# Output halves, queries and the turn of the next batch's x change their slots in a hand-written matmul schedule (gated cross-attention with a mixture feed-forward)

## What is computed

```python
q = (_layernorm(x) @ Wq + bq).reshape(B, L, NKV, G, HDIM)        # B=4, L=256, NKV=8, G=4, HDIM=128
k_, v_ = jnp.split(ctx @ Wkv + bkv, 2, axis=-1)                  # Lk=1601
scores = jnp.einsum('blkgd,bmkd->bkglm', q, k) * scale
attn = jax.nn.softmax(scores, axis=-1)
o = jnp.einsum('bkglm,bmkd->blkgd', attn, v).reshape(B, L, NHEAD * HDIM)
x = x + jnp.tanh(g_xattn[0]) * (o @ Wo + bo)
x = x + jnp.tanh(g_ffn[0]) * ffn(_layernorm(x))                  # base + top-2 of 8 LoRA adapters
```

## Time and profile before

| | |
|---|---|
| median of three runs | 2308.6 us |
| the profiled execution, its own time | 2309.07 us |
| its span | 2307.1 us |
| TensorE matmul busy | 2257.9 us, 98% |
| VectorE / ScalarE / GpSimd busy | 1812.2 / 1667.0 / 1631.9 us (79 / 72 / 71%) |
| mean granted TensorE clock | 0.999 |

### The profile page before, as it was taken

The page is one execution under the profiler, slowest core; times in us unless marked ns, Lnnn a source line. Parts: engine busy times, 40 slices in busy tenths (PEclk is TensorE's granted clock), DMA queues, the critical chain, the costliest instruction groups (busy, mean ns, idle before and its releaser), DMA issues.

```text
span 2307.1 us, 37400 instructions
## 1 busy us (share of the span) xinstructions
PE 2257.9 (98%) x12361; PEld 1940.2 (84%) x12361; DVE 1812.2 (79%) x3162; ACT 1667.0 (72%) x3156; POOL 1631.9 (71%) x1372
## 2 busy tenths in 40 slices
PE   7999999999999999999999999999999999999988
PEld 6888888887888888888888888888888888888865
DVE  5888888888787787787778787787788778787785
ACT  4777777776777777777777777777777777777763
POOL 5887886976668678757657778776756756766762
PEclk9999999999999999999999999999999999999999
DMA  7344353564233342325214333333422213222211
GB/s 259 129 158 137 118 162 110 173 202 150 88 113 110 100 159 95 128 87 202 92 49 137 111 128 120 111 130 112 160 83 96 92 60 111 67 98 88 68 66 55
DMA packets 137567, 271.85 MB, mean 118 GB/s; under 512 B 21664, under 2 KB 54944, under 8 KB 137120
## 3 DMA queue, kind: packets, MB, share of 16 engines
q1 hardware_dynamic: 122400, 255.71, 32.7%
q10 hardware_dynamic: 14976, 13.74, 2.6%
HBM read 202.44 MB, written 66.97 MB: 117 GB/s over the span
## 4 chain that ended last, share of the span: by engine, by line
PE 80%; DVE 9%; POOL 4%; issue 3%; ACT 3%; DMA 0%; ACTq 0%; SPq 0%; POOLq 0%; DVEq 0%
PE psW L419 12%; PE psW L420 12%; PE psW L421 12%; PE psS L419 7%; PE psS L421 7%; PE psS L420 7%; PE psW L616 7%; PE psW L617 6%; PE psW L618 6%; PE psW L475 3%; DVE psum_ L1309 3%; DVE mrun L1274 2%; POOL xs L805 2%; PE psW L483 1%; DVE pl L1053 1%
## 5 line engine op out<-in xcount | busy, mean ns | idle before, releaser
L805 POOL TENSOR_TENSOR xs<-xs,mb 128x512 f32<-128x512 f32 (+1 forms) x832 | 1067.8, 1309 | 475.6 <-ACT mb L876 475.6
L1274 DVE TENSOR_TENSOR mrun<-psS,mrun 128x512 f32<-128x512 f32 (+1 forms) x704 | 482.4, 685 | 339.5 <-ACT xs L876 338.3
L876 ACT ACTIVATE xs<-psS 128x512 f32<-128x512 f32 (+1 forms) x832 | 496.2, 597 | 242.6 <-PE psS L421 230.9
L1053 DVE TENSOR_TENSOR pl<-psP,ph 128x512 fp32r<-128x512 f32 (+1 forms) x672 | 459.2, 683 | 81.7 <-ACT ph L998 76.9
L998 ACT ACTIVATE ph<-xs 128x512 fp32r<-128x512 f32 (+1 forms) x832 | 518.9, 624 | 0.2 <-PE psW L618 0.2
L1309 DVE TENSOR_TENSOR psum_<-psP,psum_ 128x512 f32<-128x512 f32 (+1 forms) x672 | 456.9, 680 | 0.9 <-POOL pl L809 0.8
L995 ACT ACTIVATE psP<-xs 128x512 f32<-128x512 f32 (+1 forms) x672 | 401.2, 597 | 34.5 <-DVE rinv L1216 13.1
L419 PE MATMUL psS<-ql,kh 128*128 128x512 f32 (+1 forms) x832 | 339.4, 408 | 6.8 <-DVE mrun L1274 5.7
L616 PE MATMUL psW<-ph,vh 128*128 128x512 f32 (+1 forms) x832 | 333.9, 401 | 6.0 <-POOL pl L809 4.2
L618 PE MATMUL psW<-ph,vl 128*128 128x512 f32 (+1 forms) x832 | 328.2, 394 | 0.0
L420 PE MATMUL psS<-qh,kh 128*128 128x512 f32 (+1 forms) x832 | 328.0, 394 | 0.0
(11 more groups left out here) (188 smaller groups left out, 4377.6 us busy)
## 6 DMA issues: line engine op xcount, KB each, us to landing
wqh<-scr_wq SPq DMA_DIRECT2D x96, 256.0 KB, 2.7
wql<-scr_wq SPq DMA_DIRECT2D x96, 256.0 KB, 3.0
woh<-scr_wo SPq DMA_DIRECT2D x48, 512.0 KB, 3.3
wol<-scr_wo SPq DMA_DIRECT2D x48, 512.0 KB, 4.2
rbc<-scr_r ACTq DMA_DIRECT2D x52, 256.0 KB, 3.4
scr_wq<-wqh SPq DMA_DIRECT2D x32, 256.0 KB, 2.1
scr_wq<-wql SPq DMA_DIRECT2D x32, 256.0 KB, 2.6
scr_wo<-woh SPq DMA_DIRECT2D x16, 512.0 KB, 2.6
```

The lines of the kernel that those rows point to most:

```text
L805: eng.tensor_tensor(tile, tile, mb[0:rows_of(t), U % 2, :], ALU.subtract).then_inc(s_sub)
L876: return eng.activation(hi, src, ACT.Copy)
L1053: return eng.tensor_tensor(lo, src, f32(hi), ALU.subtract)
L1274: eng.tensor_tensor(run, psS[0:rows, s % 2, :], a, ALU.max).then_inc(s_m)
```

## The change

Three tables change. `on_slot` moves the division one slot later for V = 12, 16, 28, 32, 44, 48 and 60. The third pattern puts p0 and p1 into slots 7 and 8 (before: 4 and 7), q0 and q1 into 9 and 11 (before: 8 and 10), and drops x0 and x1; in the units with r, r stands behind p0 in slot 7. The last unit of batches 0, 1 and 2 (15, 31, 47) gets a new pattern: x0 and x1 in slots 1 and 2 (before: slots 11 and 12 of the unit before), and q0 in slot 7 (before: 1). The cuts of the query weights in units 2, 6 and 10 go to slots 10 and 12 (before: 9 and 11).

```diff
     def on_slot(V):
-        return 9 if sum_by_mem(V) else 8
+        return 9 if MEM_LO <= V < MEM_SUM else 8
...
     AT_MEM = [
         "m q0 b k3 q1 s v0 v1 v2 v3 v4 o0 o1",
         "m,v5 v6 b q0 k0 s,v7 v8 k1 q1 v9 - v10 -",
-        "m,v11 - b,v12 k2 p0 s k3 r,p1 q0 - q1 x0 o0,x1",
+        "m,v11 - b,v12 k2 - s k3 p0,r p1 q0 - q1 o0",
         "m q0 b k0 p1 s k1 - q1 k2 - o0 o1",
     ]
     TURN = "m,v11 p0 b,v12 k2 p1 s k3 r q0 - q1 - o0"
+
+    NEXT_X = "m x0 b,x1 k0 p1 s k1 q0 q1 k2 - o0 o1"
...
-                    UN - 1: "m - b - p1 s - r - - o0 - -"}.get(U, TURN if U > NU and U % NU == 2 else (AT_MEM if U >= MEM_LO + 2 else AT)[U % 4])
+                    UN - 1: "m - b - p1 s - r - - o0 - -"}.get(U, TURN if U > NU and U % NU == 2 else NEXT_X if U % NU == NU - 1 else (AT_MEM if U >= MEM_LO + 2 else AT)[U % 4])
...
         if U + 2 < NU:
-            cuts[at + (9 if u == 2 else 7)] += halves("q", 2 * U + 4)
-            cuts[at + (11 if u == 2 else 9 if u % 2 else 8)] += halves("q", 2 * U + 5)
+            cuts[at + (10 if u == 2 else 7)] += halves("q", 2 * U + 4)
+            cuts[at + (12 if u == 2 else 9 if u % 2 else 8)] += halves("q", 2 * U + 5)
```

## The result

| | before | changed |
|---|---|---|
| median of the runs | 2308.84 us (4 runs) | 2320.74 us (4 runs, 2319.5 to 2323.16) |
| span of the profiled execution | 2307.1 us | 2317.7 us |

The ratio is 1.0052, with a 95% interval of 1.004 to 1.0065: the change makes the kernel slower by 0.5%, 11.9 us by the medians, 10.6 by the spans.

The account below looks back on a forecast made before the run. TensorE, busy 98% of the span, was taken as the bound, so every new wait is paid in full. The terms summed to +10.1 on 2309.07, 2319.2; against 2318.7 from the median it said 2319.0, range 2307 to 2326.

Parts of the forecast that it names:

- D: Units 30, 46, 62 (with r): p1 waits 1.62 us for p0's bank, next scores 0.66; +4.7 us in all.
- F: Turn of x, units 14 and 15: x0's wait and low clock go, other waits come; -2.0 us, bounds -6 and +1.
- A: Slot 6 of nine third-pattern units: without p0 in slot 4, PV waits 0.44 us for GpSimd.
- B: Slot 12 of six units like 22: the old 0.74 us wait for a maximum goes, -4.4 us.
- C: q1 in slot 11, six units like 22: the next unit's first scores wait 0.96 us for its remainder.
- eight transposes move ...: nothing: Units 31 and 47: the x transposes moved in, with k0 taking x0's bank, add no wait.
- E: Units 6 and 10: GpSimd's output-weight cut waits for a later p1, PV 7.6 moves by 1.54 us; +3.1 us.
- 0.4 more at the spread b of 15.2: Unit 15, slot 2, part of F: 0.4 us more waiting because VectorE is late.
- G: Units 18, 34, 50: the later division delays block 6's `pl` by 0.1 us each; +0.3 us, bounds -0.3 and +1.
- The rule that was weighed: Idle stretches between matmul bursts lower TensorE's clock, so the waits of 1.62 and 2.2 us might cost clock again.
- the clock rival: Clock falls behind p1's wait in units 14, 30, 46, 62: 1.67 us each, +6.7, 2326 us; chance 0.07.

Follow-up runs that it names:

- e9: Changed kernel with p0 of the third pattern back in slot 4, r alone in slot 7, q0 and q1 left in 9 and 11: 2314.32 us, one run.
- e5: Changed kernel with the third pattern's p0 back in slot 4, r alone in 7, and q1 in slot 10 instead of 11: 2307.27 us.
- e2: Changed kernel with q1 of the third pattern in slot 10 instead of 11, nothing else: 2317.89 us.
- e3: Changed kernel with r ahead of p0 in slot 7 instead of behind it: 2320.65 us.
- e4: Changed kernel with the output weights' cuts three slots later in units 6, 10 and 14 (slots 8 and 9): 2316.58 us.
- e1: Kernel before with only the turn of x moved, as in the change (pattern of units 15, 31, 47): 2307.1 us.
- e7: e1 with GpSimd's normalisation of x in slot 15.0 instead of 14.8, and x0, x1 in slots 15.4 and 15.5: 2308.93 us.
- e8: e6 with another job order in units 15, 31, 47, and unit 62 in the order and division of the kernel before: 2295.73 us.
- e6: e5 with the later cut of e4 and the later normalisation and turn of e7: 2303.05 us.
- e10: Kernel before with only the division of V = 12, 16, 28, 32, 44, 48, 60 one slot later: 2308.79 us, one run.

## Why the prediction was right, point by point

The forecast was 2319.0 with 0.75 for slower; measured are 2320.74. The new waits came each with the releaser and in the slot that it named. Some of the closeness is luck: the parts came to +12.6 where they were forecast at +10.1 (D was 1.3 too low, F 1.1, the others right to 0.1), the medians differ by 11.9, and a faster unit 0 took 2.1 off the profile.

- **A** (0.44 forecast): 0.37 to 0.40 in nine units; gone in e9 and e5 with p0 in slot 4.
- **B and C** (-0.74, +0.96): the old wait is gone, the new one is 0.89; e2 takes it away, e9 keeps it without A. A, B and C make +0.53 a unit and two restarts of 0.1 make it 0.7 (forecast 0.66).
- **D** (1.62 and 0.66): 1.54 and 0.58; e3 moves the first to another releaser by the order of banks alone. The sum came out 1.3 too low (6.0 for 4.7). The term that failed is "eight transposes move ...: nothing": units 31 and 47 last 1.25 more for 0.81 of transposes, so 0.45 each was left at nothing. 0.17 of it is k0's wait for x0's bank; where the rest lies was not tried. The other 0.5 lies in units 62 and 63 (+1.7 for +1.2), where the feed-forward's first norm took 3.42 us of VectorE for 0.94 before, which the prediction did not have (last section).
- **E** (3.1): 3.0, of it 1.47 at PV 7.6. That TensorE's own waits on the way don't matter is shown by e2, whose units 6 and 7 sum to the same 70.5 us; e4 gives back 1.2 and 1.6.
- **F** (-2.0): -0.9. x0's wait and the clock are gone, p1's and q1's waits are there (1.54; 1.94 for 2.2 at the end of unit 14), unit 15 has no wait in slots 8 to 11. Two terms were mis-sized: "0.4 more at the spread b of 15.2" measured 1.22 (0.24 and 0.98), and the 0.45 of the turn as above. e1, where p1's wait is absent, has 2.08 in 15.2: the 4.15 us of normalisation, which stand before block 9, reach TensorE whether or not x0 waits for them. e7 and e8 take them out of the way and the PV wait goes.
- **G** (0.3): 0.4.

The rule that was weighed: behind the waits of 1.54 in units 14, 30, 46 and 62 the granted clock stayed full in the changed kernel's profile, and in those of e2 and e4, so the clock rival did not come about there.

## What to carry to other kernels

Where buffers go round in a first-in, first-out queue, write down for each job whose buffer it takes and in which place of the other engine's queue that one is freed: a job right behind the one whose bank it gets waits for a whole hand-over (here p1 could start only 3.0 us into its slot, 1.54 late). A result that the next stage's first step needs must leave the queue of the engine that reads it out of PSUM one slot before that step, and a helper that blocks in order on someone's output (GpSimd's cut) must have all that is due sooner in front of it. Slots chosen by these waits, with one cut and the normalisation moved too, came out 14 us below the kernel before (e8); the slots of the change came out 12 above it.

## What the runs showed of the hardware that was not expected

**The same wait, with and without a clock fall.** In unit 63 all twelve profiles have the same idle time of TensorE in slot 10, 1.42 to 1.44 us, with one of about 0.17 shortly before it. Behind it the clock went to its lower level in five of them (e1, e2, e3, e4, e6) and stayed full there in the other seven (in e7 it fell 8 us later), and the unit is 1.4 to 1.6 us longer for it. The stretch of slots 63.10 and 63.11, first of the kernel before, then of e1 (span of the stretch, busy times, and the granted clock before the DMA share):

```profile
2226.70:2233.10 6.40, 4.80 (x20) 3.32 (x20) 6.33 (x13) 4.46 (x10) 6.40 (x6) 1.00 0.01 3
```

```profile
2223.10:2231.00 7.90, 6.30 (x20) 4.37 (x20) 7.26 (x17) 4.51 (x10) 7.90 (x7) 0.78 0.01 2
```

So the same idle time of 1.4 us may or may not cost another 1.4 to 1.6, and a difference of that size between two single profiles says nothing of an edit. The four longest idle times in the units, 2.81 to 2.95 us (x0 before and in e10, q1 of unit 62 in e5 and e6), each had a clock fall that began within 1.2 us of their end.

**A VectorE operation of 0.9 to 3.4 us.** The feed-forward's first norm, one instruction on VectorE, took 0.94 us in the kernel before, 0.95 in e8, 2.79 in e5 (shown above) and 3.42 in the changed kernel; the same form took 0.53 in unit 62 where GpSimd stood idle. In the kernel before VectorE came to it in slot 62.10, beside the last subtraction of a GpSimd run. In the changed kernel it comes to it at the end of slot 62.8, with three of the run's five subtractions still under way or to come:

```profile
2198.44 3.42 DVE L1129 TENSOR_SCALAR hn<-x,mv,rstd 128x512 f32<-128x512 f32 x1
```

```profile
2195.24 6.33 POOL L807 TENSOR_TENSOR xs<-xs,mb 128x512 f32<-128x512 f32 x5
```

The run ends at 2201.57 and the norm at 2201.86. GpSimd in e5:

```profile
2182.03 6.31 POOL L807 TENSOR_TENSOR xs<-xs,mb 128x512 f32<-128x512 f32 x5
```

It ended at 2188.34, VectorE's norm at 2188.63. In all twelve profiles the norm ends 0.28 or 0.29 us behind the end of GpSimd's run, whether it started beside the run's last subtraction (0.92 to 1.54 us), beside the last two (2.39 to 2.79) or the last three (3.42 to 3.43). The Trainium skill (SBUF — State Buffer, SBUF: two separate sides) says that VectorE, in some kinds of instruction, and GpSimd share a pair of ports by an exclusive lock, and that the loser is blocked for the other's whole instruction. The trace fits that, but here VectorE waited for up to three GpSimd instructions in a row. No run moved this norm alone, so the ports as the cause are not shown.
